# Row maximum of both heads of a pair in one instruction, from products of 64 rows on either half of the array

## What is computed

```python
b, n, dim = x.shape                      # 4, 1024, 128
qkv = (normed @ w_qkv).reshape(b, n, 3, 16, 64)
q = q * 64 ** (-0.5)
sim = jnp.einsum('bhid,bhjd->bhij', q, k)
sim = jnp.where(causal_mask, -jnp.finfo(sim.dtype).max, sim)
attn = jax.nn.softmax(sim, axis=-1)
out = jnp.einsum('bhij,bhjd->bhid', attn, v)
return out.reshape(b, n, 1024) @ w_out   # heads side by side
```

## Time and profile before

| | |
|---|---|
| median of 3 runs | 1580.72 us (1578.22 to 1581.95) |
| the profiled execution | 1578.72 us |
| its span in the trace | 1577.0 us |
| mean granted TensorE clock | 0.968 |
| reductions L1135 | 512, 386.8 us busy |
| max products L1291 | 768, 250.1 us busy |
| masks L1294 | 512, 119.1 us busy |

### The profile page before, as it was taken

One profiled execution on the slowest core, in us unless ns is written; L12 is line 12 of the kernel. 1 busy time (PEld: TensorE's weight loads), 2 busy tenths in 40 slices (PEclk: granted clock), 3 DMA queues, 4 the chain that ended last, 5 costly groups with the idle time before them and its releaser, 6 DMA issues.

```text
span 1577.0 us, 33357 instructions
## 1 busy us (share of the span) xinstructions
PE 1453.9 (92%) x9130; PEld 1128.0 (72%) x9131; DVE 1076.1 (68%) x2341; ACT 1067.4 (68%) x2590; POOL 904.9 (57%) x923
## 2 busy tenths in 40 slices
PE   3569999599999999999999999999999999999998
PEld 3458888477777777777777777777777777777776
DVE  6655555458866876687658776876687668766883
ACT  2536656277776777777767777777777777777775
POOL 0761000167665766676657666766676667666766
PEclk9669999699999999999999999999999999999999
DMA  8122111111111111111111111111111111111111
GB/s 308 48 83 72 52 58 48 40 38 38 33 28 41 38 33 28 41 38 33 28 39 40 33 28 39 40 33 28 39 40 33 28 40 39 33 28 41 37 28 54
DMA packets 58807, 72.86 MB, mean 46 GB/s; under 512 B 7400, under 2 KB 44560, under 8 KB 58640
## 3 DMA queue, kind: packets, MB, share of 16 engines
q1 hardware_dynamic: 40720, 52.57, 14.0%
q10 hardware_dynamic: 13824, 9.86, 2.0%
q0 software_dynamic: 4096, 8.40, 1.8%
HBM read 20.47 MB, written 16.52 MB: 23 GB/s over the span
## 4 chain that ended last, share of the span: by engine, by line
PE 67%; DVE 6%; issue 4%; ACT 3%; DMA 1%; SPq 0%; DVEq 0%; POOLq 0%; POOL 0%; ACTq 0%
PE max_ps L1291 9%; PE score_ps L1316 8%; PE score_ps L1317 8%; PE misc_ps L1350 8%; PE head_ps L1333 7%; PE head_ps L1337 7%; PE head_ps L1335 7%; PE misc_ps L1267 3%; PE max_ps L1294 2%; PE score_ps L1319 2%; DVE q_a L1125 2%; PE misc_ps L1261 2%; ACT p_hi L1082 1%; PE misc_ps L1300 1%; PE misc_ps L1263 1%
## 5 line engine op out<-in xcount | busy, mean ns | idle before, releaser
L1033 POOL TENSOR_TENSOR p_lo<-probs,p_hi 128x512 fp32r<-128x512 f32 (+3 forms) x768 | 773.7, 1022 | 432.0 <-ACT p_hi L1082 426.2
L1082 ACT ACTIVATE probs<-score_ps 128x512 f32<-128x512 f32 (+3 forms) x768 | 375.3, 489 | 250.8 <-PE score_ps L1319 170.9
L1135 DVE TENSOR_REDUCE row_max<-max_ps 128x1 f32<-128x128 f32 (+7 forms) x512 | 386.8, 756 | 171.6 <-PE max_ps L1294 161.0
L1082 ACT ACTIVATE p_hi<-score_ps 128x512 fp32r<-128x512 f32 (+3 forms) x768 | 373.1, 486 | 0.0
L1333 PE MATMUL head_ps<-p_hi,v_hi 128*65 128x512 f32 (+3 forms) x768 | 295.6, 385 | 0.3 <-POOL p_lo L1033 0.3
L1316 PE MATMUL score_ps<-q_a,k_a 128*128 128x512 f32 (+3 forms) x768 | 267.8, 349 | 14.0 <-issue 10.9
L1317 PE MATMUL score_ps<-q_b,k_b 65*128 65x512 f32 (+3 forms) x768 | 267.3, 348 | 0.0
L1291 PE MATMUL max_ps<-k_a,q_a 128*128 128x384 f32 (+5 forms) x768 | 250.1, 380 | 16.4 <-DVE row_max L1135 12.6
L1337 PE MATMUL head_ps<-p_lo,v_hi 128*65 128x512 f32 (+3 forms) x768 | 259.4, 338 | 0.0
L1335 PE MATMUL head_ps<-p_hi,v_lo 128*64 128x512 f32 (+3 forms) x768 | 259.0, 337 | 0.0
L1316 PEld LDWEIGHTS score_ps<-q_a,k_a 128*128 128x128 f32 x768 | 145.4, 189 | 60.0 <-issue 17.4
(11 more groups left out here) (170 smaller groups left out, 2105.6 us busy)
## 6 DMA issues: line engine op xcount, KB each, us to landing
k_a<-k_a SPq DMA_DIRECT2D x64, 256.0 KB, 3.8
q_b<-q_a SPq DMA_DIRECT2D x64, 256.0 KB, 4.3
sorted_x<-zeros SPq DMA_DIRECT2D x13, 384.0 KB, 16.1
w_raw<-sorted_x SPq DMA_DIRECT2D x26, 192.0 KB, 2.5
sorted_y<-result ACTq DMA_DIRECT2D x78, 64.0 KB, 1.6
acc<-in_L_attn_x_dram SPq DMA_DIRECT2D x4, 512.0 KB, 6.9
w_raw<-in_L_ffn_W_dram ACTq DMA_DIRECT2D x1, 2048.0 KB, 23.1
q_b<-shift SPq DMA_DIRECT2D x128, 2.0 KB
```

The costliest lines, as they stand in the source:

```text
L1033: pool.tensor_tensor(p_lo[:, slot, 0:w], probs[:, slot, 0:w], p_hi[:, slot, 0:w].bitcast(F32), ALU.subtract).then_inc(p_split, 1)
L1082: ins = act.activation(p[:, (g * CH + c) % RING, 0:width], score_ps[(g * CH + c) % 2][:, 0:width], ACT.Exp, scale=SCALE)
L1135: dve.tensor_reduce(row_max[:, g % 2, t:t + 1], src, axes, ALU.max).then_inc(max_taken, 1)
```

## The change

The maximum of the two heads of a pair is taken together. The rounded q and k of head `s` now stand on partitions `HI[s]`: 0 to 63 for the first, 64 to 127 for the second; the rest of q and the copy of k on the other half. A part is a pair of products with 64 rows each, one for either head, which stand on the lower and the upper half of the array and write bank 0 and bank 1 of `max_ps`. They use the rounded q alone, so the shift comes from scores without the rest of q. Each reduction takes both banks and writes two values.

A pair has 12 parts: tiles 0 to 3 whole, tiles 4 to 7 in two halves of their keys (the half with the last keys is masked, the other goes to spare columns). After the last part DVE joins the two halves of tiles 4 to 7 by one maximum. Two parts stand in steps 8 and 10 of an even head, ten in steps 0 to 9 of an odd head, all for the next pair. Every part's products wait for the reduction of the part before. The products need the rounded q and k alone; the wait for the copies and the rests moves to the first score of the pair.

```diff
+            HI = [slice(0, HEAD), slice(HEAD, P)]
-            max_parts = [(0, 0), (1, 1), (2, 0), (3, 1), (7, None), (6, None), (5, None), (4, None)]
-            MAX_AT = [0, 1, 2, 3, 4, 6, 8, 10]
+            max_parts = ([(t, 0, (t + 1) * P, t) for t in range(GROUP)]
+                         + [(t, b * (t + 1) * P // 2, (t + 1) * P // 2, t if b else t + GROUP)
+                            for t in range(GROUP, TILES) for b in range(2)])
+            MAX_AT = [(0, 8), (0, 10)] + [(1, c) for c in range(10)]
...
-                if g + 1 < final and c in MAX_AT:
-                    order.append(("max", g + 1, MAX_AT.index(c)))
+                if (g // 2 + 1) * 2 < final and (g % 2, c) in MAX_AT:
+                    order.append(("max", g // 2 + 1, MAX_AT.index((g % 2, c))))
...
+                    def maximum(hp, p, m):
+                        t, _, w, col = max_parts[m]
+                        dve.wait_ge(max_scores, n_max(hp, p, m) + 1)
+                        dve.tensor_reduce(row_max[:, p % 2, :, col:col + 1], max_ps[:, :, 0:w], AX_X,
+                                          ALU.max).then_inc(max_taken, 1)
+                        if m == PARTS - 1:
+                            dve.wait_ge(max_taken, n_max(hp, p, m) + 1)
+                            late = row_max[:, p % 2, :, GROUP:TILES]
+                            dve.tensor_tensor(late, late, row_max[:, p % 2, :, TILES:TILES + GROUP],
+                                              ALU.max).then_inc(max_joined, 1)
...
+                    def max_scores_of(hp, p, m):
+                        i = p % 2
+                        t, k0, w, col = max_parts[m]
+                        if m == 0:
+                            pe.wait_ge(hi_done, n_batch(hp, p) * 8 + 8)
...
+                        if p or m:
+                            pe.wait_ge(max_taken, n_max(hp, p, m))
...
+                        for s in range(2):
+                            ins = pe.matmul(max_ps[:, s, 0:w], q_a[i][s][HI[s], t * P:(t + 1) * P],
+                                            k_a[i][s][HI[s], k0:k0 + w], start=True, stop=col >= TILES)
+                        if col < TILES:
+                            for s in range(2):
+                                ins = pe.matmul(max_ps[:, s, w - P:w], later[:], ident16[:], start=False, stop=True)
...
+                        if c == 0 and s == 0:
+                            pe.wait_ge(copies_done, n_batch(hp, g // 2) * 64 + 64)
+                            pe.wait_ge(lo_done, n_batch(hp, g // 2) * 4 + 4)
```

More of the change, by code:

```diff
@@ L790, in attention_and_experts @@
             later = sb(ph2, "later", [P, P], BF16)
-            row_max = sb(ph2, "row_max", [P, 2, TILES])
+            row_max = sb(ph2, "row_max", [P, 2, 2, TILES + TILES // 2])
             shift = sb(ph2, "shift", [GROUP, 2, P], F32R)
@@ L952, in copies @@
                         for s in range(2):
-                            k_hi, q_hi = k_a[i][s][0:HEAD, :].bitcast(F32), q_a[i][s][0:HEAD, :].bitcast(F32)
-                            sp.dma_start(k_a[i][s][HEAD:P, :].bitcast(F32), k_hi).then_inc(copies_done, 16)
+                            hi, other = HI[s], HI[1 - s]
+                            k_hi, q_hi = k_a[i][s][hi, :].bitcast(F32), q_a[i][s][hi, :].bitcast(F32)
+                            sp.dma_start(k_a[i][s][other, :].bitcast(F32), k_hi).then_inc(copies_done, 16)
                             sp.dma_start(q_b[i][s][0:HEAD, :].bitcast(F32), q_hi).then_inc(copies_done, 16)
@@ L1122, in project @@
                             dve.wait_ge(hi_done, n_batch(hp, p) * 8 + (n * 2 + s + 1))
-                            hi = (q_a, k_a)[n // 2][i][s][0:HEAD, cols].bitcast(F32)
-                            lo = q_a[i][s][HEAD:P, cols] if n < 2 else k_b[i][s][0:HEAD, cols]
-                            ins = dve.tensor_tensor(lo, src[s * HEAD:(s + 1) * HEAD, :], hi, ALU.subtract)
+                            hi = (q_a, k_a)[n // 2][i][s][HI[s], cols].bitcast(F32)
+                            lo = q_a[i][s][HI[1 - s], cols] if n < 2 else k_b[i][s][0:HEAD, cols]
+                            ins = dve.tensor_tensor(lo, src[HI[s], :], hi, ALU.subtract)
                         ins.then_inc(lo_done, 1)
[L1128 to L1135, removed]
+                    def maximum(hp, p, m):
[8 more added lines that the diff above has]
+                                              ALU.max).then_inc(max_joined, 1)
                     def combine(hp, part):
@@ L1269, in project @@
                         ins.then_inc(misc_ready, 1)
[L1271 to L1278, removed]
+                    def max_scores_of(hp, p, m):
[3 more added lines that the diff above has]
+                            pe.wait_ge(hi_done, n_batch(hp, p) * 8 + 8)
+                        if m == 0 and p == 0:
                             pe.wait_ge(attn_consts, CONSTS)
-                        if g or BEFORE[m] >= 0:
-                            pe.wait_ge(max_taken, n_max(hp, g, BEFORE[m]) + 1)
+                        if p or m:
+                            pe.wait_ge(max_taken, n_max(hp, p, m))
                         elif m == 0:
                             pe.wait_ge(max_taken, n_max(hp, 0, 0))
[L1286 to L1294, removed]
+                        for s in range(2):
[4 more added lines that the diff above has]
+                                ins = pe.matmul(max_ps[:, s, w - P:w], later[:], ident16[:], start=False, stop=True)
                         ins.then_inc(max_scores, 1)
@@ L1298, in shifts @@
                         dst = misc_bank(hp, u)
-                        pe.wait_ge(max_taken, n_max(hp, g, HALF_MAX[half]) + 1)
-                        pe.transpose(dst[0:GROUP, 0:P], row_max[:, g % 2, half * GROUP:(half + 1) * GROUP],
+                        if half == 0:
+                            pe.wait_ge(max_taken, n_max(hp, g // 2, GROUP - 1) + 1)
+                        else:
+                            pe.wait_ge(max_joined, n_batch(hp, g // 2) + 1)
+                        pe.transpose(dst[0:GROUP, 0:P], row_max[:, g // 2 % 2, g % 2, half * GROUP:(half + 1) * GROUP],
                                      ident[:]).then_inc(misc_ready, 1)
```

9 lines of the change are left out of this document (4 added, 5 removed).

## The result

| | before | after |
|---|---|---|
| median of the runs | 1581.34 us (1578.22 to 1589.44, 4 runs) | 1724.89 us (1715.06 to 1726.60, 4 runs) |
| the profiled execution | 1578.72 us | 1726.12 us |
| its span | 1577.0 us | 1724.4 us |
| mean granted TensorE clock | 0.968 | 0.942 |

The change makes the kernel slower: ratio 1.0886, with an interval of 1.0828 to 1.0944. The direction and the place were forecast; the size was not, 1643 us with a range of 1610 to 1708.

What follows compares the result with a forecast made beforehand. PE's order was taken as the clock of the attention stage. Heads +51 us, start +6 and exposed loads 5 made +62 on 1578.7, so 1641, and 1643 for the median; range 1610 to 1708.

Steps and rivals of the forecast that it cites:

- Change of size in the array: 64-row products among 128-row ones on PE: taken to cost nothing, by the row with 64 weight columns.
- rival C: The array drains at each size change, two a part: about 1705 us at 100 ns each, 1760 at 200; chance 0.17.
- The products: Max products on PE: a pair on different rows and banks runs at once, saving 0.96 us a head, 61 us over 64.
- Where the work sits: DVE reductions: 8 per head before; now 2 in an even head, 10 in an odd one, 10.4 us against 6.05.
- the wait: Products and reductions take turns, as every part uses both banks: a handover of 0.70 us at 448 columns.
- the heads with combine: Odd heads where reductions share DVE with combine steps: head 3 +6.5 us, head 5 +3.4, head 1 +2.5.
- Start: Before the first score: parts start 3.66 us sooner, but 12 parts of both heads come first; net +6 us.
- B: Rival: the two products of a part run one after the other, +38 on A, 1681 us, range 1660 to 1700; chance 0.17.
- A: The forecast: products at once, PE waits for DVE in odd heads; 1643 us, own range 1618 to 1660; chance 0.53.
- D: Rival: not slower, as combine steps cost less where they now stand, 48 us in all; 1576 us; chance 0.13.
- the -14: A's lower edge: no exposed weight load at all, 14 us less, along with turns 7 us cheaper.
- the -19: D's sum: no exposed load, counted as 19 us less.

Runs made afterwards that it cites:

- before_64: The kernel before with its max products cut to rows 0 to 63, all else kept: 1685.5 us, ratio 1.0659.
- full_ready: The changed kernel with max products on all 128 rows, reading q and k of the batch before so no wait is added: 1715.4 us, ratio 1.0849.
- full_ready_spread: The changed kernel with 128-row max products on the batch before's q and k, parts spread over both heads: 1650.4 us, ratio 1.0424.
- spread: The changed kernel with its 12 parts spread over steps 7 to 11 of even heads and seven steps of odd heads: 1652.7 us, ratio 1.0445.
- before_turns: The kernel before with parts 1, 2 and 3 of each head also waiting for the reduction of the part just before: 1597.3 us, ratio 1.0094.

## Why the prediction was wrong in size

**The step that failed** is "Change of size in the array": "I take nothing for it and keep the drain as a rival". The nearest row chosen was the product with 64 weight columns, which passes freely. It does not stand for 64 rows. Measured, a visit costs 0.1 us on the way in and some 0.2 us behind the products beyond their columns (0.38 us for 384 columns). Net of what full products expose too it is 0.25 us a part in a plain odd head, and 0.2 over the whole kernel (before_64: 104 us for some 500 parts). By rival C's own line (100 ns each 1705 us, 200 ns 1760) the measured time is that of some 135 ns each; that this fits is partly luck, as the line has no low clock in it.

**The products.** Right that they overlap; the 61 us on PE were never there to take, as the size takes them back. full_ready and full_ready_spread, with neither overlap nor 64 rows, are as fast as their counterparts in the total and somewhat faster in the heads. Head by head: the even head was to gain 2.0 us and gained 1.37, which is two visits of 0.3. The plain odd head was to lose 2.3 and lost 3.5; ten visits at 0.3 take 3.0 us of PE there, and PE is busy 21.37 of 21.80 us, so that much of the waiting I had worked out is now filled with PE's own time.

**Where the work sits, the wait, the heads with combine.** Right, and enough by itself to make the kernel slower: full_ready, without any 64-row product, is 8.5% slower than before, and placing the parts otherwise (spread) takes back half of the loss. Head 3 was to lose 6.5 us and loses 6.9 at its shortest (clock 0.94), head 5 3.8 for 3.4. The handover was put at 0.67 us for 384 columns with masks. In the odd head after, one reduction ends at 838.15 and the next starts at 838.90, 0.75; DVE's timeline:

```profile
837.19 0.96 DVE L1134 TENSOR_REDUCE row_max<-max_ps 128x2 f32<-128x768 f32 x1 [0.72 <-PE max_ps L1290]
838.90 0.96 DVE L1134 TENSOR_REDUCE row_max<-max_ps 128x2 f32<-128x768 f32 x1 [0.75 <-PE max_ps L1294]
```

A reduction of both banks takes what its columns give: 0.96 us for 768, where 0.95 was worked out.

**The clock** stands in the prediction for the start alone. Before, head 3 is 20.05 us at clock 1.00; after, its eight instances run from 27.0 to 30.6 us, and the one looked at has 0.83. The excess of heads 1, 3 and 4 over their own shortest instance adds up to some 30 us after and to some 4 before. That is an estimate from the lengths of the heads, not an experiment: no run held the clock and kept the waits. The mean clocks bound it: 0.942 of 1724.4 us is some 200 us at half clock, 0.968 of 1577.0 some 100, and 100 us more at half clock can cost 50 at most.

**Start.** Net +6 us forecast; the first score starts at 326.03 us against 314.92, 11.1 later. Of that 4.2 were there before the max parts began (the v projection starts at 297.86 instead of 293.63), so 6.9 are the parts'.

```profile
297.86 3.78 PE L1272 MATMUL misc_ps<-w_raw,nT 128*128 128x128 f32 x16 [0.69 <-DVE k_b L1128]
...
326.03 0.77 PE L1322 MATMUL score_ps<-q_a,k_a 128*128 128x512 f32 x1 [2.20 <-DMA q_b<-shift]
```

**The sum again**, with what was measured: four even heads and head 6's wait for DVE about -4 us for eight heads, odd heads 3.5 + 6.9 + 3.8 + 3.5 = 17.7 with each at its shortest, times 8 less the last one: about 106 us; start 11, clock 25 to 30: 142 to 147, against 147.4 between the two profiled executions. Against the forecast of 62 that is 4 us more in each eight for the even heads (32 in all) and 3 more for the odd ones (24), 5 for the start and 25 to 30 for the clock, less the 5 taken for loads. So the size of the array part, at nothing in the prediction, and the clock carry most of what was missing.

**The rivals.** B's mechanism is out (the products overlap); that its time, 1681, is nearer than A's is luck, as it too gave up most of what the overlap was to bring. C was right as a mechanism and too low in chance; that a row of another kind spoke against it was no reason for 0.17. D is out: the combine steps cost the same where they stand now (of those in the earlier trace rows, 2.21 us for 2.33 and 2.16 for 2.16) and did more harm, not less. Its comparison was not of like with like: 2.33 us is a TENSOR_SCALAR, the adds of 0.87 are SCALAR_TENSOR_TENSOR. A's lower edge, 1618, does not follow from the -14 beside it (1643 - 14 - 7 = 1622); with the -19 that D uses it would be 1617. The range missed since C's upper part, and the clock on top of it, were left out.

**What stays open.** Why a single part more in turn costs what it does when other work lies between. In before_turns the plain odd head keeps its 18.31 us; of the 18 us between the profiled executions about 6 are in heads 2, 4 and 6, 6 in heads 0 and 1, which differ from one eight to the next before too, 3 in the last head 6 and 3 in the start. In full_ready_spread the clock is a small part: its mean of 0.966 over 1648.6 us is some 11 us more at half clock than before, 6 us of time at most. How the rest of its 55 us in the heads splits is not known.

## What to carry to other kernels

Two half-height products at once save the columns of one of them, and pay a visit of the other array size. Here that lost 0.06 us a part at 384 columns and was nearly even at 448. Many products of 64 rows in a row, before full ones return, would pay the visit once; no run here tried it. Fewer, larger instructions for the second engine are no gain if they double the buffer each holds: with one buffer the engines take turns, and then it matters where the other work of that engine stands, and not only how much there is; moving 21 small steps brought more here than the masks that were dropped.

## What the runs showed of the hardware

- Two products of 64 rows on the two halves of the array run fully at once: 0.44 us for a pair of 384 columns, against 0.60 for a pair of full ones.
- Going from 128 to 64 rows delays the next product by 0.1 us, and what follows a pair of them starts about 0.2 us later than their columns give. The weights of the first 64-row product are not loaded beside the product before it, as those of a full one are (815.29 against 775.54). For rows that agrees with what the Trainium skill states in "TensorEngine Tiling (Array Packing)", Key Properties, that a change of the tiling mode drains TensorE. Going from 65 to 64 weight columns costs nothing that shows; whether that changes the mode at all, no run here tells.
- PE's granted clock fell to half in short stretches behind waits for DVE: 0.57 and 0.53 in two windows of 4 and 7 us of head 3 (749 to 753 and 759 to 766 us), after waits of 1.42 us (to 748.43) and 1.48 us (to 757.37).
